# Second attention: the output product and its transposes spread over four groups, the expert weights loaded in eight parts

## Chip, cores and metric

The kernel runs on one NeuronCore of a Trainium2 chip, as one launch. The time is the device time of the whole program in microseconds (us), the median over runs. Before the change it is 1635.58 us (three runs, 1625.13 to 1639.85).

## The reference: what is computed

Two transformer-like layers run over x of shape (4 batches, 512 tokens, 256 channels), float32. Layer 0 is a modulated attention, a Mamba block and a quantised linear layer. Layer 1 is a softmax attention with 16 heads of 16 channels, and then a mixture of eight experts (hidden size 512, all experts computed for every token). The change sits in the attention of layer 1, and in the load of the expert weights that the last part needs:

```python
qkv = x @ Wqkv                       # x: the conditioned input, (4, 512, 256)
...
attn = jnp.einsum('bqhd,bkhd->bhqk', q, k)
attn = jax.nn.softmax(attn, axis=-1)
z = jnp.einsum('bhqk,bkhd->bqhd', attn, v)
z = z.reshape(b, s, d)
return z @ Wo                        # "output product"; added to x
...
h = gelu(einsum('nd,edh->neh', xf, w1) + b1)     # experts
y = einsum('neh,ehd->ned', h, w2) + b2
```

## The kernel before, in words

Each engine has its own instruction stream, written out by hand, and the engines meet at semaphores. Nothing reorders the work: what stands where in each stream is the schedule. PE is the matrix engine (matmuls and transposes into PSUM, whose eight banks are `ps[:, 0..7, :]`), ACT and DVE work on what PE made, SP issues the transfers, POOL prepares values.

The second attention goes batch by batch (`b` 0 to 3), and in each batch by four groups of four heads (`hg` 0 to 3; `g = 4 b + hg`). A group has eight steps (`j` 0 to 7), and in each step PE does, in `attend`:

- two transposed score products for this group (L1329, into banks 3 to 5), of which ACT makes exponentials (`weigh`, L1845);
- two plain score products for the group after next (L1275, banks 0 to 2), of which DVE takes row maxima (`follow`, L2285);
- after every second step, and once at the group's end, the product of exponentials and values, `values` (L1287, bank 6). The last one of a group, in the text "the group's last value product", waits for the group's last exponential. ACT copies its result to SBUF (L1859) before it begins the next group's exponentials.

Bank 7 is shared by everything small. In each group it holds: at j = 2 the maxima turned into a row (`max_rows`, L1144), which ACT copies to `mrow` (L1835) and SP sends with a small transfer into the score operand (L772, "the row of maxima"); at j = 5 the previous group's result turned to rows (`z_rows`, L1296), which DVE normalises (L2289, L2291) at its step s = 11 of 16. PE waits for the row of maxima at the start of the next group (semaphore `max_row_in_stack`).

When all four groups of a batch are done, its output product follows, during the next batch: the normalised result is transposed in two halves (`zn_columns`, L1305), each copied by ACT (L1850) to `zn_t`; then two products with `Wo` (`attention_out`, L1312), each added to x by DVE (`attention_add`, L2297). All of these go through bank 7 too. Before the change all of it is done in the group hg = 1 of the next batch, which in the text is called **the loaded group**; a group without any of it is **a plain group**. The last batch has its first transposed half in its own last group, and the rest behind the attention.

SP's stream (`feed`) sends per group the row of maxima and then, when the group's last transposed score product is done, twelve loads of heads for the next batch (L632, 64 KB each), and in batch 0 at hg = 2 one transfer of the expert weights (L780, `fw[:, cut_at:]`, 128 partitions x 16384 floats, 8.39 MB). Batches 1 and 2 are one hardware loop on every engine. The experts' stage, behind the attention, begins with waits for these weights (L1374, L2318).

## Time and profile before

| what | value |
|---|---|
| median of three runs | 1635.58 us (1625.13 to 1639.85) |
| the profiled execution's own time | 1633.18 us |
| span of the profiled execution | 1631.4 us |
| PE busy | 1454.8 us, 89% of the span |
| ACT busy, DVE busy | 855.9 us, 1067.1 us |
| share of the DMA engines taken by the transfers | 15.7% |
| second attention | about 935.7 to 1187.8 us |
| expert stage | from about 1213 us to the end |

The page gives the whole program. The change touches only the second attention, so the rows below come from queries on that stretch: instructions in order of time on one engine, with the idle time before them in square brackets and what ended it; and busy time, granted clock of PE and DMA traffic in chosen stretches. The expert stage and all before 935 us have the same instructions in both kernels.

### The profile page before, as it was taken

The page shows a single profiled execution, that of the slowest core. Times are in us where ns is not written, and L with a number is a line of the kernel's source. Part 1 is how long each engine was busy: PE and PEld are TensorE (multiplying, and loading weights), DVE is VectorE, ACT ScalarE, POOL GpSimd, SP SyncE. Part 2 cuts the span into 40 slices and gives each one's busy share as a digit, 9 for nine tenths or more (in the row PEclk, how much of TensorE's full clock was granted, in tenths as well). Part 3 has the DMA queues.
Part 4 walks back from the last instruction along what each step waited for, and adds up shares of the span by engine and source line. Part 5 has one row for each costly group of instructions (what it writes and reads, how often), then busy time and mean ns, then how long its engine had stood idle before and what let it go on. Part 6 is the DMA issues. An engine that isn't in the chain of part 4 may idle for free.

```text
span 1631.4 us, 20342 instructions
## 1 busy us (share of the span) xinstructions
PE 1454.8 (89%) x7408; PEld 994.1 (61%) x7420; DVE 1067.1 (65%) x1216; ACT 855.9 (52%) x1511; POOL 477.4 (29%) x140
## 2 busy tenths in 40 slices
PE   5898797589898989989998796889899999999997
PEld 3666342388797979643444332333258888888886
DVE  6995586589898988763344575667364565465655
ACT  2432465599898998532333385668734333333332
POOL 0998210079798888200333210000000000000000
PEclk7899998799999999978999998999998999999999
DMA  6100011302322211410203036112000000000000
GB/s 263 56 25 1 1 52 59 137 31 88 117 89 93 79 52 52 146 21 20 58 39 107 20 94 241 48 42 56 1 1 0 1 14 1 1 13 1 13 1 13
DMA packets 35616, 87.61 MB, mean 54 GB/s; under 512 B 8238, under 2 KB 24836, under 8 KB 32836
## 3 DMA queue, kind: packets, MB, share of 16 engines
q1 hardware_dynamic: 35524, 86.39, 15.7%
q8 instruction: 57, 0.93, 0.2%
q14 instruction: 35, 0.29, 0.1%
HBM read 68.10 MB, written 18.21 MB: 53 GB/s over the span
## 4 chain that ended last, share of the span: by engine, by line
PE 53%; ACT 3%; DVE 2%; issue 2%; DMA 1%; DVEq 1%; ACTq 0%
PE ps L1412 12%; PE ps L1421 12%; PE ps L1287 4%; PE ps L1154 3%; PE ps L1329 3%; PE ps L1275 2%; PE ps L1180 2%; PE ps L1116 2%; ACT arena L1845 2%; PE ps L986 1%; DMA arena<-mrow 1%; PE ps L580 1%; PE ps L1312 1%; PE ps L1038 1%; PE ps L1188 1%
## 5 line engine op out<-in xcount | busy, mean ns | idle before, releaser
L2494 POOL TENSOR_TENSOR arena<-arena 128x2048 f32<-128x2048 f32 x63 | 287.3, 4583 | 168.5 <-DVE arena L2053 168.1
L2053 DVE TENSOR_TENSOR_SCAN arena<-arena,ps 128x1024 f32<-128x1024 f32 x128 | 284.2, 2272 | 45.0 <-ACT arena L1688 22.4
L1412 PE MATMUL ps<-arena 128*128 128x256 f32 x896 | 215.5, 387 | 3.3 <-DVE early L2439 1.9
L1412 PEld LDWEIGHTS ps<-arena 128*128 128x128 f32 x896 | 172.2, 193 | 30.0 <-DVE early L2439 3.1
L1845 ACT ACTIVATE arena<-ps,rho 128x512 f32<-128x512 f32 x256 | 158.2, 689 | 59.3 <-PE ps L1329 58.3
L1688 ACT ACTIVATE arena<-arena,mam 128x511 f32<-128x511 f32 x256 | 166.2, 712 | 34.1 <-DVE arena L2053 34.1
L2285 DVE TENSOR_REDUCE mxs<-ps 128x1 f32<-128x512 f32 x224 | 141.2, 684 | 58.8 <-PE ps L1275 57.0
L974 PE MATMUL ps<-early,arena 128*128 128x128 f32 x768 | 129.7, 277 | 18.3 <-DVE arena L2053 17.9
L1878 ACT ACTIVATE hT<-hT,arena 128x256 f32<-128x256 f32 x192 | 85.7, 502 | 86.4 <-DVE hT L2443 54.9
L2474 POOL TENSOR_TENSOR arena<-arena 128x4096 f32<-128x4096 f32 x16 | 115.0, 7190 | 43.6 <-DVE arena L1972 43.6
L1676 ACT ACTIVATE arena<-arena,early 128x512 f32<-128x512 f32 x192 | 124.1, 711 | 0.1
L986 PE MATMUL ps<-early,arena 128*128 128x128 f32 x1024 | 121.5, 272 | 0.9 <-POOL arena L2494 0.7
L1421 PE MATMUL ps<-hT,arena 128*128 128x256 f32 x512 | 121.2, 380 | 0.0
L986 PEld LDWEIGHTS ps<-early,arena 128*128 128x128 f32 x1024 | 113.5, 140 | 1.8 <-POOL arena L2494 1.0
L1329 PE MATMUL ps<-arena 97*128 97x512 bf16 x256 | 96.9, 387 | 17.7 <-DMA arena<-mrow 13.5
L974 PEld LDWEIGHTS ps<-early,arena 128*128 128x128 f32 x768 | 90.5, 142 | 32.0 <-DVE arena L2053 22.9
L1421 PEld LDWEIGHTS ps<-hT,arena 128*128 128x128 f32 x512 | 97.7, 191 | 13.4
L1878 ACT ACTIVATE hT<-ps,arena 128x256 f32<-128x256 f32 x64 | 26.9, 471 | 138.9 <-PE ps L1412 138.9
L975 PE MATMUL ps<-arena 128*128 128x128 f32 x512 | 99.4, 276 | 0.0
L1421 PE MATMUL ps<-mam,arena 128*128 128x256 f32 x384 | 93.3, 379 | 0.0
L2439 DVE TENSOR_TENSOR early<-mam,ps 128x512 f32<-128x512 f32 x32 | 22.0, 687 | 101.1 <-PE ps L1412 101.1
L1275 PE MATMUL ps<-arena 96*128 96x512 bf16 x224 | 86.1, 384 | 0.0
(344 smaller groups left out, 2318.7 us busy)
## 6 DMA issues: line engine op xcount, KB each, us to landing
arena<-bc_scratch SPq DMA_DIRECT2D x32, 512.0 KB, 3.7
batch_scratch<-arena SPq DMA_DIRECT2D x2, 3072.0 KB, 9.1
arena<-batch_scratch SPq DMA_DIRECT2D x6, 1024.0 KB, 6.9
arena<-q_scratch SPq DMA_DIRECT2D x96, 64.0 KB, 2.2
arena<-k_scratch SPq DMA_DIRECT2D x96, 64.0 KB, 2.2
arena<-in_dec_w SPq DMA_DIRECT2D x1, 3855.0 KB, 16.3
arena<-in_cond SPq DMA_DIRECT2D x1, 3739.5 KB, 11.4
arena<-in_ids SPq DMA_DIRECT2D x4, 768.0 KB, 7.9
```

The costliest lines, as they stand in the source:

```text
L974: pe.transpose(ps[:, FEED + m, t * P:(t + 1) * P], dub[:, k % 2, t, m * P:(m + 1) * P], ident)
L986: last = pe.matmul(ps[:, t, m * P:(m + 1) * P], state[:, k % SLOTS, m, t * P:(t + 1) * P], ident, start=False, stop=(k % NS == NS - 1 and ...
L1275: pe.matmul(ps[:, (hg + s) % 3, :], q[0:STACK, i, qc * P:(qc + 1) * P], k[0:STACK, i, :], start=True, stop=True).then_inc(s_s_mm, 1)
L1329: pe.matmul(ps[:, 3 + (hg + n) % 3, :], k[0:STACK + 1, i, kc * P:(kc + 1) * P], q[0:STACK + 1, i, :], start=True, stop=True).then_inc(s_t_ ...
L1412: done = pe.matmul(ps[:, bank, i * S // 2:(i + 1) * S // 2], weights[:, f, :], x, start=first and i == 0, stop=last and i == 1, skip_group ...
L1421: done = pe.matmul(ps[:, bank, half * S // 2:(half + 1) * S // 2], weights[:, f, :], x[:, i, :], start=(r == 0 and half == 0 and i == 0), ...
L1676: act.activation(dub[:, k % 2, t, :], duT[b % 2][:, t, :], ACT.Copy, scale=bt[:, b, t, n:n + 1])
L1688: last = act.activation(decay[:, (2 * k + h) % 3, i, 1:S], dt[b % 2][:, m, 1:S], ACT.Exp, scale=a_neg[:, m * NS + n:m * NS + n + 1])
L1845: act.activation(pt[:, j % 4, i], ps[:, 3 + (hg + n) % 3, :], ACT.Exp, scale=rho[:, 0:1]).then_inc(s_pt, 1)
L2053: dve.tensor_tensor_scan(half, view(decay[:, (2 * k + h) % 3], [[1, 2 * S]]), view(ps[:, FEED + 2 * h, :], [[1, 2 * S]]), 0.0, ALU.mult, A ...
L2285: dve.tensor_reduce(mxs[:, hg % 2, qc, i:i + 1], ps[:, (turn + s) % 3, :], AX, ALU.max).then_inc(s_max, 1)
L2494: pool.tensor_tensor(state[:, k % SLOTS], state[:, k % SLOTS], view(c_rows[:, j % 2, k % G, :], [[0, M], [1, S]]), ALU.mult).then_inc(s_hc, 1)
```

## The change

Five things are different.

1. The output product of a batch and its transposes are spread over four groups, each at j = 7, between the group's last scores and its last value product: the first transposed half at hg = 3 of the batch itself, the second at hg = 0 of the next batch, the two products with `Wo` at hg = 1 and hg = 2. In the last batch's last group the first half stays at j = 2.
2. ACT's two copies of the transposed halves move to j = 0 of hg = 0 and hg = 1 (behind the first two exponentials), and DVE's two additions to s = 2 of hg = 2 and hg = 3 (behind the third maximum).
3. PE's waits at j = 2, 3, 5 and 7 follow: each use of bank 7 waits for the one before it.
4. The expert weights come as eight transfers of 128 x 2048 floats (1.05 MB), one behind the twelve loads of heads of each group of batches 1 and 2. The waits at the expert stage count to eight of them.
5. SP's stream is written out for all four batches instead of a loop for batches 1 and 2. The other engines keep their loop.

The diff:

```diff
@@ block.sync @@
             cut_at = FFN["w1"][0]
+            EW_LOADS = (B - 2) * HG
+            EW_PART = (FFN_W - cut_at) // EW_LOADS
...
                     if not last:
                         sp.wait_ge(s_t_mm, g * 16 + 16)
-                        if isinstance(b, int) and hg == 0:
+                        if b == 0 and hg == 0:
                             sp.wait_ge(s_q_out, 16 * B + 1)
                             sp.wait_ge(s_k_out, 16 * B + 1)
                         load_heads(sp, b + 1, hg, Q_STACK, K_STACK)
-                        if isinstance(b, int) and hg == HG - 2:
-                            sp.dma_start(fw[:, cut_at:], t_in["ffn"][:, cut_at:]).then_inc(s_ew, 16)
-
-            feed(0, False)
-            with sp.Fori(1, B - 1) as b:
-                feed(b, False)
-            feed(B - 1, True)
+                        if 1 <= b < B - 1:
+                            part = slice(cut_at + ((b - 1) * HG + hg) * EW_PART, cut_at + ((b - 1) * HG + hg + 1) * EW_PART)
+                            sp.dma_start(fw[:, part], t_in["ffn"][:, part]).then_inc(s_ew, 16)
+
+            for b in range(B):
+                feed(b, b == B - 1)
@@ block.tensor, attend @@
                         if j % 2 == 0 and j:
                             values(b, hg, kc - 1)
-                        if j < 2 and hg == 1 and not first:
-                            zn_columns(b - 1, j)
                         if j == 2 and final and hg == HG - 1:
+                            pe.wait_ge(s_x3, b * C + 1)
                             zn_columns(b, 0)
                         elif j == 2:
-                            if hg == 1 and not first:
-                                pe.wait_ge(s_znt, b * C + 1)
-                            elif not (first and hg == 0):
+                            if not first:
+                                if hg < 2:
+                                    pe.wait_ge(s_znt, b * C + hg)
+                                else:
+                                    pe.wait_ge(s_x3, (b - 1) * C + hg)
+                            elif hg:
                                 pe.wait_ge(s_zn, g)
                             max_rows(b + (hg + 1) // HG, (hg + 1) % HG)
-                        if j in (3, 4) and hg == 1 and not first:
-                            pe.wait_ge(s_mrow, g + 3)
-                            attention_out(b - 1, j - 3)
                         if j == 5 and not (first and hg == 0):
                             if not (final and hg == HG - 1):
                                 pe.wait_ge(s_mrow, g + 3)
                             else:
                                 pe.wait_ge(s_znt, b * C + 2)
-                            if hg == 1:
-                                pe.wait_ge(s_x3, b * C + 1)
                             z_rows(*((b, hg - 1) if hg else (b - 1, HG - 1)))
+                        if j == 7 and hg == 0 and not first:
+                            zn_columns(b - 1, 1)
+                        if j == 7 and hg in (1, 2) and not first:
+                            pe.wait_ge(s_zn, g + 1)
+                            attention_out(b - 1, hg - 1)
+                        if j == 7 and hg == HG - 1 and not final:
+                            pe.wait_ge(s_zn, g + 1)
+                            zn_columns(b, 0)
                     values(b, hg, TILES - 1)
...
-            pe.wait_ge(s_ew, 16)
+            pe.wait_ge(s_ew, 16 * (B - 2) * HG)
@@ block.scalar, weigh @@
-                        if hg == 1 and j in (1, 2) and not first:
-                            act.wait_ge(s_zn_tr, (b - 1) * C + j)
+                        if hg < 2 and j == 0 and not first:
+                            act.wait_ge(s_zn_tr, (b - 1) * C + hg + 1)
                             act.wait_ge(s_wo_mm, (b - 1) * C + 1)
-                            act.activation(zn_t[:, j - 1, :], ps[:, 7, :], ACT.Copy).then_inc(s_znt, 1)
+                            act.activation(zn_t[:, hg, :], ps[:, 7, :], ACT.Copy).then_inc(s_znt, 1)
@@ block.vector, follow @@
-                        if s in (7, 9) and hg == 1 and not first:
-                            attention_add(b - 1, (s - 7) // 2)
+                        if s == 2 and hg >= 2 and not first:
+                            attention_add(b - 1, hg - 2)
...
-            dve.wait_ge(s_ew, 16)
+            dve.wait_ge(s_ew, 16 * (B - 2) * HG)
```

How this moves instructions is shown at three places. In these rows the names in brackets are the semaphores waited for. The first is SP's stream from the end of group 1 of batch 0. Before:

```order
L772 DMA arena<-mrow 1x4x512
L632 DMA arena<-q_scratch 16x4x512 x6
L632 DMA arena<-k_scratch 16x4x512 x6
L780 DMA arena<-in_ffn 128x16384
L772 DMA arena<-mrow 1x4x512
L632 DMA arena<-q_scratch 16x4x512 x6
L632 DMA arena<-k_scratch 16x4x512 x6
```

and the change, from the row of maxima behind the loads of group 2 of batch 0 up to the second part of the weights:

```order
L774 DMA arena<-mrow 1x4x512
L632 DMA arena<-q_scratch 16x4x512 x6
L632 DMA arena<-k_scratch 16x4x512 x6
L774 DMA arena<-mrow 1x4x512
L632 DMA arena<-q_scratch 16x4x512 x6
L632 DMA arena<-k_scratch 16x4x512 x6
L783 DMA arena<-in_ffn 128x2048
L774 DMA arena<-mrow 1x4x512
L632 DMA arena<-q_scratch 16x4x512 x6
L632 DMA arena<-k_scratch 16x4x512 x6
L783 DMA arena<-in_ffn 128x2048
```

The one transfer of 128 x 16384 between two rows of maxima is gone; from batch 1 on, a part of 128 x 2048 stands behind each twelve loads and ahead of the next row of maxima.

The second is PE in the group hg = 1 of the loop body, around the first product with `Wo` (L1312 before, L1313 now). Before, it stands behind j = 3, its bank released by ACT's copy of the row of maxima:

```order
L1327 REGISTER_ALU
L1329 MATMUL ps<-arena 128x512 [waits exp_scores_ready]
L1273 REGISTER_ALU
L1275 MATMUL ps<-arena 128x512 [waits max_ready]
L1346 REGISTER_ALU
L1310 REGISTER_ALU [waits zn_copied,max_row_ready]
L1312 MATMUL ps<-hT,arena 128x512 [waits x3_ready]
L1312 MATMUL ps<-hT,arena 128x512
L1327 REGISTER_ALU
L1329 MATMUL ps<-arena 128x512 [waits exp_scores_ready]
```

Now it stands behind the last scores of the group (j = 7), ahead of the group's last value product (L1288) and the first score of the next group:

```order
L1328 REGISTER_ALU
L1330 MATMUL ps<-arena 128x512 [waits exp_scores_ready]
L1274 REGISTER_ALU
L1276 MATMUL ps<-arena 128x512 [waits max_ready]
L1311 REGISTER_ALU [waits zn_copied,z_normalised]
L1313 MATMUL ps<-hT,arena 128x512 [waits x3_ready]
L1313 MATMUL ps<-hT,arena 128x512
L1282 REGISTER_ALU
L1288 MATMUL ps<-arena 32x512 [waits exp_scores_ready]
L1288 MATMUL ps<-arena 32x512 x3
L1330 MATMUL ps<-arena 128x512 [waits exp_scores_ready,max_row_in_stack]
```

It moved from the middle of the group to its end, and its bank is now released by DVE's normalisation (`z_normalised`).

The third is ACT at the start of the last batch, groups 0 and 1 (the copies to `zn_t` are L1850 before, L1856 now; L1859 and L1865 copy the value product). Before, both copies are in group 1:

```order
L1845 ACTIVATE arena<-ps,rho 128x512 [waits value_products,scoreT_products] x8
L1835 ACTIVATE mrow<-ps 4x512 [waits max_row_in_stack,max_transposed]
L1845 ACTIVATE arena<-ps,rho 128x512 [waits value_products,scoreT_products] x8
L1859 ACTIVATE hT<-ps 128x512 [waits z_transposed,value_products]
L1845 ACTIVATE arena<-ps,rho 128x512 [waits value_products,scoreT_products] x4
L1850 ACTIVATE hT<-ps 128x512 [waits attention_out_products,zn_transposed]
L1845 ACTIVATE arena<-ps,rho 128x512 [waits value_products,scoreT_products] x2
L1850 ACTIVATE hT<-ps 128x512 [waits attention_out_products,zn_transposed]
L1845 ACTIVATE arena<-ps,rho 128x512 [waits value_products,scoreT_products] x2
L1835 ACTIVATE mrow<-ps 4x512 [waits max_row_in_stack,max_transposed]
```

and now there is one in each of the two groups, behind two exponentials:

```order
L1851 ACTIVATE arena<-ps,rho 128x512 [waits value_products,scoreT_products] x2
L1856 ACTIVATE hT<-ps 128x512 [waits attention_out_products,zn_transposed]
L1851 ACTIVATE arena<-ps,rho 128x512 [waits value_products,scoreT_products] x6
L1841 ACTIVATE mrow<-ps 4x512 [waits max_row_in_stack,max_transposed]
L1851 ACTIVATE arena<-ps,rho 128x512 [waits value_products,scoreT_products] x8
L1865 ACTIVATE hT<-ps 128x512 [waits z_transposed,value_products]
L1851 ACTIVATE arena<-ps,rho 128x512 [waits value_products,scoreT_products] x2
L1856 ACTIVATE hT<-ps 128x512 [waits attention_out_products,zn_transposed]
L1851 ACTIVATE arena<-ps,rho 128x512 [waits value_products,scoreT_products] x6
```

One of the two copies moved a group earlier, and both stand ahead of the third exponential.

## Rows read from the trace of the kernel before

**Rows 1.** Page, part 1: the span.

```profile
span 1631.4 us, 20342 instructions
```

**Rows 2.** Busy time by stretch: the second and third batch of the attention.

```profile
core 0: us, PE busy (x) PEld busy (x) DVE busy (x) ACT busy (x) POOL busy (x), PEclk, DMA share, GB/s
...
988.80:1066.70 77.90, 58.66 (x309) 20.12 (x306) 43.87 (x74) 44.64 (x74) 1.61 (x4) 0.89 0.29 97
1066.70:1127.90 61.20, 55.51 (x308) 18.95 (x304) 43.58 (x74) 44.15 (x74) 1.61 (x4) 1.00 0.19 52
```

**Rows 3.** PE in order of time, around the stall.

```profile
987.82 1.07 PE L1287 MATMUL ps<-arena 128*32 128x512 f32 x8 [0.70 <-ACT arena L1845]
1002.43 0.61 PE L1329 MATMUL ps<-arena 97*128 97x512 bf16 x1 [13.55 <-DMA arena<-mrow]
```

**Rows 4.** SP's DMA queue in order of time; blocks of loads and single rows.

```profile
979.05 0.42 SPq L780 DMA_DIRECT2D arena<-in_ffn  x1
982.12 0.58 SPq L772 DMA_DIRECT2D arena<-mrow  x1
...
1054.34 2.72 SPq L632 DMA_DIRECT2D arena<-k_scratch  x6
1059.96 0.60 SPq L772 DMA_DIRECT2D arena<-mrow  x1
```

**Rows 5.** DMA issues: KB each, median us to landing (attention).

```profile
arena<-q_scratch SPq DMA_DIRECT2D x78, 64.0 KB, 2.1
...
arena<-in_ffn SPq DMA_DIRECT2D x1, 23.0
```

**Rows 6.** Busy time by stretch: the output product after the stall.

```profile
1026.00:1030.00 4.00, 3.71 (x5) 1.37 (x6) 0.00 (x0) 0.17 (x1) 0.00 (x0) 0.57 0.00 1
```

**Rows 7.** PE in order of time: the end and start of plain groups.

```profile
1065.66 1.06 PE L1287 MATMUL ps<-arena 128*32 128x512 f32 x8 [0.70 <-ACT arena L1845]
1066.66 0.39 PE L1329 MATMUL ps<-arena 97*128 97x512 bf16 x1
...
1069.80 1.07 PE L1287 MATMUL ps<-arena 128*32 128x512 f32 x8
```

**Rows 8.** PE in order of time: the loaded group of the third batch.

```profile
1079.10 1.06 PE L1287 MATMUL ps<-arena 128*32 128x512 f32 x8 [0.70 <-ACT arena L1845]
...
1080.98 0.60 PE L1305 MATMUL ps<-early,hT 128*128 128x128 f32 x4
1081.42 0.38 PE L1329 MATMUL ps<-arena 97*128 97x512 bf16 x1
...
1083.69 0.66 PE L1305 MATMUL ps<-early,hT 128*128 128x128 f32 x4 [1.23 <-ACT hT L1850]
...
1086.56 0.60 PE L1144 MATMUL ps<-early,mxs 128*4 128x128 f32 x4 [0.35 <-ACT hT L1850]
...
1089.27 1.98 PE L1312 MATMUL ps<-hT,arena 128*128 128x512 f32 x4 [1.24 <-ACT mrow L1835]
1091.09 0.38 PE L1329 MATMUL ps<-arena 97*128 97x512 bf16 x1
```

**Rows 9.** ACT in order of time: a group's start.

```profile
1066.80 0.60 ACT L1859 ACTIVATE hT<-ps 128x512 f32<-128x512 f32 x1 [1.19 <-PE ps L1287]
1067.33 3.58 ACT L1845 ACTIVATE arena<-ps,rho 128x512 f32<-128x512 f32 x6
```

**Rows 10.** DVE in order of time: idle after six maxima, then an addition.

```profile
1071.87 2.48 DVE L2285 TENSOR_REDUCE mxs<-ps 128x1 f32<-128x512 f32 x4 [0.88 <-PE ps L1275]
...
1091.39 0.69 DVE L2297 TENSOR_TENSOR xT<-ps,xT 128x512 f32 x1 [2.47 <-PE ps L1312]
```

**Rows 11.** PE in order of time: ends of groups, last batch.

```profile
1126.95 1.07 PE L1287 MATMUL ps<-arena 128*32 128x512 f32 x8 [0.70 <-ACT arena L1845]
...
1161.12 1.07 PE L1287 MATMUL ps<-arena 128*32 128x512 f32 x8 [0.70 <-ACT arena L1845]
...
1173.88 1.06 PE L1287 MATMUL ps<-arena 128*32 128x512 f32 x8 [1.14 <-ACT arena L1845]
...
1186.75 1.06 PE L1287 MATMUL ps<-arena 128*32 128x512 f32 x8 [1.14 <-ACT arena L1845]
```

## Prediction, on record before the changed kernel ran

> **What bounds the kernel now.** I read the second attention in four steps. First its batches as stretches of busy time: the second and the third do the same work, but the second is longer, at a mean granted clock of 0.89 against 1.00 and with 97 GB/s of transfers against 52 [rows 2]. The reader is to see that something happens to the second that is not its work. Then PE in order of time: one wait of 13.55 us for a transfer of the row of maxima [rows 3], and, in the loaded group, waits of 1.23, 0.35 and 1.24 us for ACT [rows 8], which plain groups don't have. Then SP's queue, which tells why the row was late. Then ACT and DVE in order of time at the start of a group, where the moved instructions land.
>
> **Plain groups.** I measure a group from the start of one last value product to the next. 1065.66 to 1079.10 is 13.44 us [rows 7, 8]. PE waits in it in two places: 0.70 us ahead of the last value product, for ACT's last exponential, and from the start of the group, 1066.66, to the first value product, 1069.80, it goes at ACT's pace: ACT copies the value product (its next instruction starts 0.53 us later) and makes the exponentials at some 0.6 us each (six in 3.58 us) [rows 7, 9]. Between, from 1069.80 on, PE has no idle. So whatever delays the first four exponentials delays the group, and PE has 0.70 us free at its end.
>
> **Part 1, the weights in eight parts.** The 8.39 MB transfer starts at 979.05 and takes 23.0 us; the row of maxima is issued at 982.12, behind it, and PE gets it at 1002.43 [rows 3, 4, 5]. Batch 1 runs from 987.82 to 1065.66, 77.84 us; batch 2 from 1065.66 to 1126.95, 61.29 us [rows 3, 7, 11]. The difference, 16.55 us, is the stall of 13.55 us and what it does to PE's clock: PE begins again at the lower level (0.63 us where 0.39 is usual) and has the lower level once more in 1026 to 1030, mean 0.57 [rows 3, 6, 7]. All 16.55 us should go. What comes in its place: eight parts of 1.05 MB, at the same rate 23.0 / 8 = 2.9 us each. In the stretch 1054 to 1060 the last six loads of a block are issued until 1054.34 + 2.72 = 1057.06; the part would go out there (its issue takes 0.42 us), be through by about 1060 to 1061, and the row of maxima is issued at 1059.96 [rows 4]. PE needs that row at 1066.66 [rows 7], 6.7 us after its issue; a 64 KB load lands in 2.1 us [rows 5], so some 4 us are left. SP is busy 0.42 us longer in a gap of 1059.96 - 1057.06 = 2.9 us. I take 0 for the eight waits. Their bounds are 0 and 2.0 us each, worked out with a part that moves at the pace of the head loads around it (twelve of 64 KB issued in 2 x 2.72 = 5.4 us, some 145 GB/s, so 7.2 us for a part): it is through at 1064.3, the row lands at 1066.4 or, with one more load's landing, 2.1 us later, at 1068.5. 0 is nearer to the row of the big transfer, which is of the same kind. The last part goes out at the end of batch 2 and has the whole last batch, some 55 us, before anyone waits for it: 0. The heads of the next batch stand ahead of the part in their block, and are behind no part but the one of the group before, which is through long before: 0.
>
> Of the split the Trainium skill has a rule that speaks against it: "DMA: Bandwidth & Descriptors", section "Anatomy of one DMA", gives each transfer a fixed cost of about 2.0 us beside its bytes, whatever its size. By it seven more transfers are 14 us more, and if they stood on the path the gain would be an estimated 15 us instead of the 29 of the sum below. The trace shows the landing time (2.1 us) but also that loads of 64 KB are issued six in 2.72 us, so they overlap.
>
> **Part 2, what leaves the loaded group.** It costs 61.29 - 4 x 13.44 = 7.5 us per batch over four plain groups. Of this, PE's own work is 2 x 0.44 us for the transposes (1080.98 to 1081.42) and 2 x 1.82 us for the products (1089.27 to 1091.09), 4.5 us; the other 3.0 us are the three waits, 1.23 + 0.35 + 1.24 = 2.82 [rows 8], and small change.
>
> **Part 3, what the four groups get instead.** The two transposes, 0.44 us each, now stand in the 0.70 us in which PE is free ahead of the last value product: 0. The two products, 1.82 us each, stand in the same place: 0.70 hidden, 1.12 left, 2.24 us per batch. The last value product is that much later, and behind it ACT's copy and the next group's exponentials, all by the same 1.12 us, so it is counted once. ACT's two copies stand ahead of the third exponential, where PE goes at ACT's pace: 0.53 us each (the copy of the value product, the nearest row [rows 9]), 1.06 us per batch, not hidden; the bounds are 0, if ACT's idle later in the group gave it back, and 0.63. DVE's additions, 0.69 us [rows 10], stand behind the third maximum; DVE has 0.88 us idle behind the sixth, and the maxima that it delays are needed three products later: 0, bounds 0 and 0.69. The new waits: those at j = 2 are for a copy or an addition that stands five steps of ACT or DVE earlier than PE's seventh score product; the one at j = 7 is for a normalisation that DVE begins at step 11 of 16, with three maxima behind it that PE's last score product needs anyway. 0 for both. A batch then takes 4 x 13.44 + 2.24 + 1.06 = 57.06 us.
>
> **The last batch** runs from 1126.95 to 1186.75, 59.80 us [rows 11]. Its last two groups have no score products ahead and take 1173.88 - 1161.12 = 12.76 and 12.87 us, with 1.14 us free at the end. Now: 13.44 + 0.53, then 13.44 + 0.53 + 1.12, then 12.76 + (1.82 - 1.14 = 0.68), then 12.87, in all 55.37 us.
>
> **The sum.** Batch 1: 77.84 - 57.06 = 20.8. Batch 2: 61.29 - 57.06 = 4.2. Last batch: 59.80 - 55.37 = 4.4. Together 29.4 us, of which 16.55 from the weights and 12.9 from the spreading. The profiled execution took 1633.18 us, 1.8 us more than its span of 1631.4 [rows 1]; 1633.2 - 29.4 = 1603.8. The median of the runs shown is 2.4 us above the profiled one, and they differ among themselves by 15 us, so I add nothing for it beyond rounding: **1604 us**.
>
> **The rivals.**
>
> *Forecast, 0.68:* both parts work as priced, 1597 to 1612 us. The width is the bounds of part 3, -3.2 us for the copies and +4.1 us for six additions of 0.69, and what the clock does by chance.
>
> *The spreading gives nothing, 0.12.* ACT is as near to being the bound as PE: at each group's start PE waits for it, and the products now delay ACT's copy of the value product. If PE starts each such group with a wait and the copies cost twice their time (the exponentials behind them lose the overlap), the 12.9 us shrink to between 0 and 5: 1612 to 1617 us. Against it: the order in a group is the same for all engines from the last value product on, so a delay there should not grow.
>
> *More than forecast, 0.12.* The copies are hidden (3.2 us) and half of the rest of the products too, 1593 to 1597 us; or the execution has one drop of the clock less outside the attention.
>
> *Each transfer's landing is on the path, 0.04.* The row of maxima waits for the landing of the part ahead of it, and the slack of 4 us is not there. Seven landings of 2.1 us [rows 5] are 14.7 us: 1619 us. It is what the fixed cost in the Trainium skill's "DMA: Bandwidth & Descriptors" would do here. The overlap of the head loads speaks against it.
>
> *Slower than before, 0.04.* The row of maxima is behind a part in each of eight groups, where it was behind one transfer once. From the row's issue PE can wait 6.7 us without harm. If the parts, mixed with the head loads of 16 x 4 pieces, are so slow that the row lands 15 us after its issue, each group stalls 8.3 us, 66 us in all, against 29: 1670 us. The point from which it decides is a landing 10.4 us after the issue (29.4 / 8 = 3.7 us of stall each). For it: this very wait did happen. Against it: it took eight times the bytes, and of the 20.2 us between the row's issue and PE's start almost all was the big transfer.
>
> **How the numbers follow.** The range reaches from the better case to the case in which the spreading gives nothing: **1594 to 1618 us**, which leaves out some 0.1 to 0.15. A measurement of this kernel can tell about 1% (16 us) from no change; faster by over 1% is below 1619 us. That takes in the first three cases and half of the fourth: 0.93. Within 1%: 0.04. Slower: 0.03.
>
> **What the changed profile would show.** The wait of PE for the row of maxima is gone or below 1 us in all groups, and the granted clock is 1.00 throughout the attention. The weights land as eight transfers in about 3 us each (with the queue ahead of them perhaps 5). Plain groups still take 13.4 us; groups with hg = 1 about 15.1, hg = 2 about 14.6, hg = 0 about 14.0, hg = 3 about 13.4. The waits for the copies ahead of L1306 and L1145 and for the row copy ahead of L1313 are gone; the 0.70 us ahead of the last value product is gone in hg = 1 and 2 and shorter in hg = 0 and 3. The expert stage takes what it took. The prediction would be wrong if the row of maxima is waited for in the groups of batches 1 and 2, if the groups with a product grow by more than 1.8 us, or if the expert stage waits for its weights.

## Result, and the profile after

The changed kernel takes **1610.86 us** (median of four runs, 1609.13 to 1615.05) beside 1637.28 us for the kernel before on the same chip (four runs, 1625.13 to 1639.85): a ratio of 0.9868, 95% interval 0.9819 to 0.9917. It was measured twice more among the experiments, at 1603.47 us (0.9823, 0.9797 to 0.9850) and 1603.38 us (0.9846, 0.9804 to 0.9887). The forecast was 1604 us in a range of 1594 to 1618.

The first profiled execution of it took 1612.12 us, against 1633.18 before. Page, part 1:

```profile
span 1610.3 us, 20214 instructions
...
PE 1461.8 (91%) x7408; PEld 999.7 (62%) x7420; DVE 1066.7 (66%) x1216; ACT 855.1 (53%) x1511; POOL 477.2 (30%) x140
```

The span is 21.1 us shorter than before [rows 1], where the sum of the forecast was 29.4. Where the missing 8 us are is read from six stretches of both kernels: batch 0 from its first score product, batches 1 to 3 each from last value product to last value product, from there to the layer's modulated product (L1396 before, L1402 after), and the rest. Of the kernel before (columns: stretch and its length, busy time of each engine with its instructions, granted clock, share of the DMA engines, GB/s):

```profile
935.70:987.80 52.10, 49.30 (x276) 16.32 (x276) 41.32 (x70) 42.27 (x71) 6.88 (x8) 1.00 0.43 137
...
1126.90:1186.70 59.80, 49.78 (x272) 16.20 (x272) 26.53 (x47) 43.74 (x74) 0.40 (x1) 1.00 0.05 14
1186.70:1198.20 11.50, 10.56 (x44) 5.63 (x45) 9.65 (x11) 1.19 (x2) 0.00 (x0) 1.00 0.01 2
1198.20:1631.40 433.20, 421.63 (x1921) 363.29 (x1919) 240.20 (x374) 145.31 (x305) 0.00 (x0) 0.98 0.02 6
```

(Batches 1 and 2 are [rows 2], whose stretches begin 1 us later.) And of the change:

```profile
938.00:992.50 54.50, 52.20 (x280) 17.39 (x280) 41.74 (x70) 42.75 (x71) 6.85 (x8) 0.95 0.26 74
992.50:1049.00 56.50, 55.01 (x304) 19.23 (x304) 43.40 (x75) 43.81 (x75) 1.60 (x4) 1.00 0.37 113
1049.00:1105.50 56.50, 55.06 (x304) 19.23 (x304) 43.38 (x75) 43.83 (x74) 1.60 (x4) 1.00 0.43 131
1105.50:1161.70 56.20, 50.51 (x268) 16.09 (x268) 26.50 (x47) 43.42 (x74) 0.40 (x1) 0.97 0.11 34
1161.70:1175.50 13.80, 13.75 (x44) 6.93 (x45) 9.44 (x11) 1.19 (x2) 0.00 (x0) 0.75 0.01 2
1175.50:1610.30 434.80, 423.31 (x1921) 364.63 (x1919) 240.48 (x374) 145.01 (x305) 0.00 (x0) 0.97 0.02 6
```

The three batches take 169.2 instead of 198.9 us, 29.75 less, where the forecast had 29.4. They begin and end at these value products:

```profile
992.57 1.06 PE L1288 MATMUL ps<-arena 128*32 128x512 f32 x8 [0.26 <-ACT arena L1851]
...
1161.75 1.06 PE L1288 MATMUL ps<-arena 128*32 128x512 f32 x8 [1.14 <-ACT arena L1851]
```

But batch 0 takes 54.5 us at a mean clock of 0.95 instead of 52.1 at 1.00, though its work is the same but for one transposed half at its end, and the first score product had come 2.3 us late before it; the stretch behind the last batch takes 13.8 instead of 11.5 us at 0.75; and the rest 434.8 instead of 433.2. That is 2.3 + 2.5 + 2.3 + 1.6 = 8.7 us given back, in stretches whose instructions the change does not touch, but for that half. The 2.5 us of batch 0 are all in its first group, 14.38 us in place of 11.91. In all the profiles of this document the first score product stands anywhere between 929.65 and 938.00 us, behind the same code, so the 2.3 us are within that scatter.

The first two groups of batch 1, on PE in order of time. The rows of L1288 that are quoted are the groups' last value products; in between stands the product with `Wo`:

```profile
1006.45 1.06 PE L1288 MATMUL ps<-arena 128*32 128x512 f32 x8 [0.26 <-ACT arena L1851]
...
1019.25 0.38 PE L1276 MATMUL ps<-arena 96*128 96x512 bf16 x1
1019.47 1.88 PE L1313 MATMUL ps<-hT,arena 128*128 128x512 f32 x4
1021.28 1.06 PE L1288 MATMUL ps<-arena 128*32 128x512 f32 x8
1022.28 0.39 PE L1330 MATMUL ps<-arena 97*128 97x512 bf16 x1
```

L1313 begins as soon as the last score product is issued, 1.81 us go by, and the value product follows without idle. What stood ahead of it before, 0.70 us of idle [rows 7], is used up. The group takes 1021.28 - 1006.45 = 14.83 us. The row of maxima is no longer waited for. In SP's queue the part stands between the loads and the row, which is issued at 1014.63 and needed at 1022.28:

```profile
1008.25 2.77 SPq L632 DMA_DIRECT2D arena<-k_scratch  x6
1011.06 0.43 SPq L783 DMA_DIRECT2D arena<-in_ffn  x1
1014.63 0.58 SPq L774 DMA_DIRECT2D arena<-mrow  x1
```

and the eight parts land in 4.9 us each, in the median (DMA issues, KB each, us to landing):

```profile
arena<-in_ffn SPq DMA_DIRECT2D x8, 1024.0 KB, 4.9
```

ACT at the start of batch 1, where a copy of a transposed half (L1856) stands behind two exponentials:

```profile
993.70 0.60 ACT L1865 ACTIVATE hT<-ps 128x512 f32<-128x512 f32 x1 [1.19 <-PE ps L1288]
994.19 1.26 ACT L1851 ACTIVATE arena<-ps,rho 128x512 f32<-128x512 f32 x2
995.33 0.61 ACT L1856 ACTIVATE hT<-ps 128x512 f32<-128x512 f32 x1
995.81 2.44 ACT L1851 ACTIVATE arena<-ps,rho 128x512 f32<-128x512 f32 x4
```

The next exponential starts 0.48 us after the copy.

### The profile page after: what moved, and what is told of

Read it like the earlier page. It is cut to its first block, busy times and chain, and to the rows that moved or that the text cites. A ratio compares the mean times of both kernels' runs of the same rounds, so it can differ in the third digit from the quotient of the medians.

```text
span 1610.3 us, 20214 instructions
## 1 busy us (share of the span) xinstructions
PE 1461.8 (91%) x7408; PEld 999.7 (62%) x7420; DVE 1066.7 (66%) x1216; ACT 855.1 (53%) x1511; POOL 477.2 (30%) x140
## 4 chain that ended last, share of the span: by engine, by line
PE 55%; ACT 2%; DVE 2%; issue 2%; DVEq 1%; ACTq 0%
PE ps L1418 13%; PE ps L1427 12%; PE ps L1288 4%; PE ps L1155 3%; PE ps L1330 3%; PE ps L1276 2%; PE ps L1181 2%; PE ps L1117 2%; ACT arena L1851 1%; PE ps L987 1%; PE ps L580 1%; PE ps L1313 1%; PE ps L1039 1%; PE ps L1189 1%; PE ps L1167 1%
## 5 line engine op out<-in xcount | busy, mean ns | idle before, releaser
L1851 ACT ACTIVATE arena<-ps,rho 128x512 f32<-128x512 f32 x256 | 158.3, 689 | 27.7 <-PE ps L1330 26.5
## 6 DMA issues: line engine op xcount, KB each, us to landing
arena<-in_dec_w SPq DMA_DIRECT2D x1, 3855.0 KB, 16.4
arena<-in_cond SPq DMA_DIRECT2D x1, 3739.5 KB, 11.5
```

The costliest lines, as they stand in the source:

```text
L1851: act.activation(pt[:, j % 4, i], ps[:, 3 + (hg + n) % 3, :], ACT.Exp, scale=rho[:, 0:1]).then_inc(s_pt, 1)
```

## Experiments

Times are medians of six runs beside the kernel before on the same chip, or a single run where the text says so; a single run has no interval. A trace shows one of a kernel's runs, not its median. "Attention" is the time from the end of batch 0 to the end of the last batch, the three batches that the change is about; for the kernel before it is 198.93 us and for the change 169.18.

**parts_only: the weights in eight parts, the output product left in the loaded group.**

```diff
 # the kernel before, with the change's SP stream and its counts:
-                        if isinstance(b, int) and hg == HG - 2:
-                            sp.dma_start(fw[:, cut_at:], t_in["ffn"][:, cut_at:]).then_inc(s_ew, 16)
...
+                        if 1 <= b < B - 1:
+                            ...
+                            sp.dma_start(fw[:, part], t_in["ffn"][:, part]).then_inc(s_ew, 16)
...
-            pe.wait_ge(s_ew, 16)
+            pe.wait_ge(s_ew, 16 * (B - 2) * HG)
...
-            with sp.Fori(1, B - 1) as b:
-                feed(b, False)
+            for b in range(B):
+                feed(b, b == B - 1)
```

> The weights in eight parts alone; the output product stays in the loaded group. Theory A (the two parts of the change add up, and what is missing from the forecast is the clock outside the attention): the stall of 13.5 us and its clock loss go, batch 1 takes 61.3 us like batch 2, 16.5 us less in the attention, about 1620 us. Rival B (the eight parts cost something by their landings): batches 1 and 2 take over 62 us each, 1624 us or more.

1614.63 us, ratio 0.9898 (0.9871 to 0.9925). The ends of batch 0 and of the last batch:

```profile
984.94 1.07 PE L1288 MATMUL ps<-arena 128*32 128x512 f32 x8 [0.70 <-ACT arena L1846]
...
1167.27 1.06 PE L1288 MATMUL ps<-arena 128*32 128x512 f32 x8 [1.14 <-ACT arena L1846]
```

Attention 182.33 us, 16.60 less than before, where the forecast had 16.55. Batches 1 and 2 take 61.24 and 61.28 us. Rival B falls. (This edit also writes SP's loop out; one_late_load below, which is written out too and has one transfer, has the wait, so it is not the writing out that removes it.)

**spread_only: the output product spread, the weights as one transfer in batch 0.**

```diff
 # the change, with SP's stream of the kernel before:
-                        if 1 <= b < B - 1:
-                            ...
+                        if isinstance(b, int) and hg == HG - 2:
+                            sp.dma_start(fw[:, cut_at:], t_in["ffn"][:, cut_at:]).then_inc(s_ew, 16)
...
 # (and the loop for batches 1 and 2 and the counts of 16 as before)
```

> The spreading alone; the weights come as one transfer in batch 0 as before. Theory A: the stall of 13.5 us is still there, batches 2 and 3 take 56.4 us each, 13 us less in the attention than before, 1624 us. Rival C (the spreading brings a drop of the granted clock behind the attention, about 3.5 us, that the kernel before did not have): 1628 us, with the drop between the last group and the modulated product of layer 1 in this kernel and not in the one with the parts alone.

1610.33 us, ratio 0.9855 (0.9819 to 0.9891). Attention 182.53 us, with a wait of 12.86 us for the row of maxima:

```profile
1003.67 0.60 PE L1329 MATMUL ps<-arena 97*128 97x512 bf16 x1 [12.86 <-DMA arena<-mrow]
```

Further, batch 2 takes 56.49 us, the last 54.83. Batch 0 takes 54.57 us. From the end of the last batch to the modulated product it takes 13.82 us, as with the change, and behind that 426.50 us, 6.6 less than before. The attention takes 16.4 us less, not 13: batch 1 has 71.21 us where it had 77.84, which is 1.7 to 1.8 us more than the other batches gained (4.8 and 5.0), because no second drop of the clock followed the stall (its hg = 1 takes 14.84 us); and the other batches gained more than expected. The median is 14 us below the 1624 expected. In the trace, whose run took 1614.35 us, the gain of 18.8 us over the profile of before is made of 16.4 in the attention, 6.6 behind the modulated product and 0.5 ahead of the attention, less 2.5 in batch 0 and 2.3 behind the last batch. That the median is another 4 us lower no trace explains. As for rival C: the drop behind the last group is in this kernel (13.82 us) and not in the one with the parts alone (11.50), as it has it.

**after_again: the change once more.** No edit.

> The changed kernel once more, unaltered. Theory A (drops of the clock in the unchanged code are chance): the drop at the attention's start (4.5 us by the value product of the first group) and the one behind its last group (3.4 us) are there in some executions only; 1610 us. Rival C: the drop behind the last group is there again, and none at the start.

1603.47 us, ratio 0.9823 (0.9797 to 0.9850). Its profile, of a run of 1609.00 us, the slowest of the six, has the same drops as the first: 54.59 us in batch 0, 14.74 us in hg = 2 of the last batch where 13.26 is its time at full clock (spread_only), 13.81 us behind the last batch. At this point rival C stood better than theory A, also for the start: the four profiles with the spreading (with copy_later below) had 54.6 us in batch 0, the two without had 52.1.

**copy_later: ACT's two copies one step later.**

```diff
-                        if hg < 2 and j == 0 and not first:
+                        if hg < 2 and j == 1 and not first:
```

> As the change, but ACT's copies of the transposed halves stand one step later (j = 1, behind the fourth exponential instead of the second). Theory A: PE's first value product of the group waits for the fourth exponential only, and the copy then runs beside that product's 1.0 us; the 0.5 us per copy go, groups hg = 0 take 13.4 instead of 13.9 us and hg = 1 14.3 instead of 14.8, 3 us less than the change in all, 1608 us. Rival D (ACT is the bound of the whole group): the copy costs the same 0.5 us wherever it stands, 1611 us.

1602.44 us, ratio 0.9796 (0.9756 to 0.9836), against 1603.47 for the change on the same chip: no difference that the intervals allow. But the attention takes 166.37 us instead of 169.2, each with one drop of the clock in the last batch, and it has the expected mechanism. Behind the last batch it has no drop (11.51 us). PE in order of time, groups hg = 3 of batch 0 and hg = 0 of batch 1:

```profile
988.93 1.06 PE L1288 MATMUL ps<-arena 128*32 128x512 f32 x8 [0.26 <-ACT arena L1851]
...
993.02 1.07 PE L1288 MATMUL ps<-arena 128*32 128x512 f32 x8
994.02 0.60 PE L1145 MATMUL ps<-early,mxs 128*4 128x128 f32 x4
...
1002.32 1.06 PE L1288 MATMUL ps<-arena 128*32 128x512 f32 x8 [0.26 <-ACT arena L1851]
```

The group takes 1002.32 - 988.93 = 13.39 us, a plain group's time, where the change takes 13.88. The first value product comes 4.09 us after the group's mark in place of 4.58, and `max_rows` (L1145) follows it at once. On ACT the copy now stands behind four exponentials (L1851), and it is done within that value product:

```profile
990.06 0.60 ACT L1865 ACTIVATE hT<-ps 128x512 f32<-128x512 f32 x1 [1.19 <-PE ps L1288]
990.55 2.41 ACT L1851 ACTIVATE arena<-ps,rho 128x512 f32<-128x512 f32 x4
992.83 0.62 ACT L1856 ACTIVATE hT<-ps 128x512 f32<-128x512 f32 x1
993.31 1.30 ACT L1851 ACTIVATE arena<-ps,rho 128x512 f32<-128x512 f32 x2
994.87 1.26 ACT L1851 ACTIVATE arena<-ps,rho 128x512 f32<-128x512 f32 x2 [0.26 <-PE ps L1330]
```

The copy's 0.48 us is taken from ACT's idle time ahead of the seventh exponential, 0.26 us where the plain group has 0.74. Rival D falls.

**one_late_load: the weights as one transfer, in batch 1.**

```diff
-            EW_LOADS = (B - 2) * HG
+            EW_LOADS = 1
...
-                        if 1 <= b < B - 1:
+                        if 1 <= b < B - 1 and ((b - 1) * HG + hg) % 8 == 0 and ((b - 1) * HG + hg) // 8 < EW_LOADS:
...
 # (which leaves b = 1, hg = 0; the two counts follow)
```

> As the change, but the weights come as one transfer of 8.39 MB, behind the loads of batch 1, hg = 0. Theory A (the row of maxima waits because it stands behind the big transfer in SP's queue, whatever the batch): PE waits some 13 us for the row at the start of the third group of batch 1, with clock loss about 15 us more than the change in the attention. Rival E (the stall of the kernel before came from the store and load traffic of batch 0): no wait.

One run, 1619.05 us. PE waits for the row of maxima at the start of the group after next, as expected:

```profile
1033.56 0.61 PE L1331 MATMUL ps<-arena 97*128 97x512 bf16 x1 [12.34 <-DMA arena<-mrow]
```

The transfer lands in 24.6 us. The attention takes 182.15 us, 13.0 more than with eight parts, where 15 were expected. Rival E falls: it is the long transfer ahead of the row, not batch 0.

**four_parts: parts of 2.1 MB in every other group.**

```diff
-            EW_LOADS = (B - 2) * HG
+            EW_LOADS = 4
...
+                        if 1 <= b < B - 1 and ((b - 1) * HG + hg) % 2 == 0 and ((b - 1) * HG + hg) // 2 < EW_LOADS:
...
 # (the two counts follow)
```

> As the change, but four parts of 2.1 MB, one in every other group of batches 1 and 2. The part goes out 9.6 us before PE needs the row of maxima behind it; at the rate of the single transfer (8.39 MB in 23.0 us) it takes 5.8 us, at that of the eight parts (1.05 MB in 4.9 us) 9.8 us. Theory A: no wait of PE for the row, groups as in the change (13.4 to 14.8 us). Rival F (a part lands as slowly per byte as the eight did, and the landing of the row comes on top): a wait of some 2 us in each of four groups.

One run, 1609.99 us. Attention 169.16 us and no wait, the same as with eight. Each part lands in 7.3 us, between the two rates:

```profile
arena<-in_ffn SPq DMA_DIRECT2D x4, 2048.0 KB, 7.3
```

With 1.05 MB in 4.9, 2.1 MB in 7.3 and 8.39 MB in 24.6 us, the landing is, by an estimate from these three, some 2.0 to 2.5 us (the head loads still ahead of it in the queue among them) and 2.3 to 2.8 us per MB. Between a part's issue and the need for the row stand 9.8 us at the least here (a part in hg = 2) and 9.6 with eight; 7.3 of them are taken here and 4.9 with eight parts. Rival F falls.

**filler: idle score products in the last two groups.**

```diff
                             if not (final and hg >= 2):
                                 scores(*ahead, n)
+                            elif n >= 2:
+                                if hg == 2 and n == 2:
+                                    pe.wait_ge(s_max, B * HG * 16 + 1)
+                                pe.matmul(ps[:, (hg + n) % 3, :], q[0:STACK, i, kc * P:(kc + 1) * P], k[0:STACK, i, :],
+                                          start=True, stop=True)
```

> As the change, and in the last batch's groups hg = 2 and 3, where no score products are ahead, PE does 28 plain score products whose results nobody reads. Rival C, in its stronger form (the clock drops behind the attention because these two groups and what follows leave PE idle too often): the drops of the last batch (1.4 us in hg = 2, 2.3 us between the last group and the modulated product) go, at the price of up to 1.3 us of PE work: 2.4 us less in the stretch from the end of batch 2 to the modulated product. Theory A (the drops are chance): they are there or not as in the change, and the stretch is 1.3 us longer when they are.

These are 14 products in each of the two groups, 28 in all. 1597.33 us, ratio 0.9799 (0.9762 to 0.9836). The drop in hg = 2 is not there (14.35 us with the filler; 13.26 without filler and drop), but it was not there without the filler either, in spread_only and one_late_load. The one behind the last group is longer: 15.35 us to the modulated product in place of 13.8, and from the end of batch 2 to that product it takes 71.9 us, 1.8 more than in the change. The stronger form of rival C falls there. The rest takes 426.45 us, 8.3 less than with the change.

**mid_products: the products with Wo at j = 3.**

```diff
-                        if j == 7 and hg in (1, 2) and not first:
-                            pe.wait_ge(s_zn, g + 1)
+                        if j == 3 and hg in (1, 2) and not first:
+                            pe.wait_ge(s_mrow, g + 3)
                             attention_out(b - 1, hg - 1)
...
+                            if hg in (1, 2) and not first:
+                                pe.wait_ge(s_x3, (b - 1) * C + hg + 1)
                             z_rows(*((b, hg - 1) if hg else (b - 1, HG - 1)))
...
-                        if s == 2 and hg >= 2 and not first:
-                            attention_add(b - 1, hg - 2)
+                        if s == 7 and hg in (1, 2) and not first:
+                            attention_add(b - 1, hg - 1)
```

> As the change, but the two products with Wo stand at j = 3 of hg = 1 and hg = 2 (behind the copy of the row of maxima) instead of j = 7, and DVE's additions at s = 7 of the same groups. Theory A (what a product costs is set by whether it fills the 0.7 us that PE is free ahead of the last value product): each costs its whole 1.82 us and the wait for the row copy, 1.2 us: hg = 1 takes 16.9 and hg = 2 16.4 us instead of 14.8 and 14.3. Rival G (the place does not matter, only that there is one use of the bank per group): 14.8 and 14.3 us.

One run, 1608.30 us. hg = 1 takes 17.09 us and hg = 2 16.54 (16.9 and 16.4 were expected). The new wait ahead of the previous group's rows costs PE no idle. Batch 1, hg = 1, on PE:

```profile
1003.52 1.07 PE L1288 MATMUL ps<-arena 128*32 128x512 f32 x8
...
1007.23 1.98 PE L1313 MATMUL ps<-hT,arena 128*128 128x512 f32 x4 [1.23 <-ACT mrow L1843]
...
1016.04 1.07 PE L1288 MATMUL ps<-arena 128*32 128x512 f32 x8 [0.70 <-ACT arena L1853]
```

The product waits 1.23 us for the row copy, costs its whole 1.8, and the 0.70 us ahead of the last value product stay empty. A product costs 16.54 - 13.40 = 3.14 us here and 0.94 at j = 7. Rival G falls: having only one extra use of bank 7 in a group is not enough, the place counts.

**before_again: the kernel before once more.** No edit.

> The kernel before, once more, for its drops of the granted clock outside the attention. Theory A (the drop at the attention's start is chance): from the first score to the end of batch 0 it takes 52.1 us or 54.6 us; either may come. Rival H (the drop at the start comes only with some of the kernels): 52.1 us again.

One run, 1630.46 us. Batch 0 takes 52.12 us, which both theory A and rival H allow. The attention takes 196.77 us, with a wait of 12.55 us for the row of maxima. In this execution the second drop of the clock after the stall (1026 to 1030 in the first, [rows 6]) did not come: the loaded group of batch 1 takes 21.04 us, not 22.75. And behind the last batch:

```profile
981.70:1057.40 75.70, 57.46 (x304) 19.70 (x304) 43.93 (x75) 44.73 (x75) 1.61 (x4) 0.91 0.32 112
...
1178.50:1193.80 15.30, 15.26 (x44) 7.76 (x45) 9.56 (x11) 1.20 (x2) 0.00 (x0) 0.67 0.01 2
1193.80:1628.70 434.90, 423.34 (x1921) 364.57 (x1919) 240.35 (x374) 145.06 (x305) 0.00 (x0) 0.97 0.02 6
```

15.3 us at a mean clock of 0.67, longer than in any profile of the change. So the drop behind the attention does not need the spreading.

**after_third: the change a third time.** No edit.

> The changed kernel a third time, for comparison on one chip with the next two. 1603 us by the second measurement, 1611 by the first. In its profile 169.2 us from the end of batch 0 to the end of the last batch, 13.8 us from there to the modulated product and 434.7 us behind it if the drops of the clock there are tied to the kernel (rival C); if they are chance (theory A), at least one of the last two numbers differs.

1603.38 us, ratio 0.9846 (0.9804 to 0.9887). This profile has neither the drop at the start nor the one in the last batch:

```profile
931.80:983.90 52.10, 49.74 (x280) 16.86 (x280) 41.24 (x70) 42.26 (x71) 6.91 (x8) 1.00 0.27 77
...
1096.90:1151.70 54.80, 48.88 (x268) 15.82 (x268) 26.48 (x47) 43.44 (x74) 0.40 (x1) 1.00 0.11 34
1151.70:1165.50 13.80, 13.71 (x44) 6.93 (x45) 9.45 (x11) 1.23 (x3) 0.00 (x0) 0.75 0.01 2
1165.50:1600.30 434.80, 423.34 (x1921) 364.62 (x1919) 240.33 (x374) 145.09 (x305) 0.00 (x0) 0.97 0.02 6
```

Batch 0 takes 52.1 us, the last batch 54.8 in place of 56.2, the attention 167.83 us. The two numbers that the expectation named are unchanged (13.81 and 434.70), so by its wording theory A is not borne out there; by the start and the last batch it is. Rival H is not borne out either: the change has had both 54.6 and 52.1 us at the start.

**filler_again and copy_filler**, beside after_third on one chip. copy_filler has the edits of filler and of copy_later.

> The kernel with the 28 idle score products in each of the last two groups, a second time, beside the change on one chip. If its gain of about 6 us over the change (1597.3 against 1603.5 on another chip) is its own, it is there again, with 426.5 us behind the modulated product instead of 434.7. If it was the chip or chance: both kernels within 2 us.

1604.64 us, ratio 0.9828 (0.9790 to 0.9866). Against 1603.38 for the change: within 2 us. The gain of 6 us did not come again, though the profile again has 426.4 us behind the modulated product, and 15.35 us ahead of it.

> Both: ACT's copies behind the fourth exponential, and the idle score products in the last batch. The copies save 3 us in the attention (measured there: 13.4 and 14.3 us for hg = 0 and 1). If both gains add: 1594 us, the fastest of all. If the clock behind the attention takes the gain back, as it did in part for the kernel with the later copies alone (1602.4 us): 1598 to 1602 us.

1603.85 us, ratio 0.9824 (0.9784 to 0.9864); one of its six runs took 3757 us, and what disturbed it is not known. The median of the other five is 1601.30. The 1594 us of the first case did not come; the 1598 to 1602 of the second fits those five. The attention takes 166.58 us against 169.44 in filler_again, hg = 0 and hg = 1 take 13.40 and 14.35 us. The 3 us of the copies are there in the trace, and not to be told from nothing in the medians. Behind the last batch it has 11.50 us, without a drop, and then 434.73. No version beats the change by more than the measurement can tell.

## Why the prediction was right

**Part 1, the weights.** Forecast 16.55 us, measured 16.60 (parts_only). Some luck is in this agreement: both are taken against the first profile of before, whose batch 1 has a second drop of the clock of 1.7 us behind the stall [rows 6]. The other three profiles with a stall (before_again, spread_only, one_late_load) don't have it, and against before_again the weights are worth 75.70 - 61.24 = 14.5 us. The cause, a small transfer issued behind a long one, is shown from both sides: the wait is there with one transfer in batch 0 (before, spread_only) and in batch 1 (one_late_load), and gone with four or eight parts. What of the long transfer holds the row up is not shown. All these transfers go through SP's one queue, and the DMA engines are about full as well (by the profile a mean share of 0.84 to 1.15 in each stretch of 5 to 6 us from 979 to 1002 in the kernel before). Whether the row would have come in time through another engine's queue was not tried. The parts landed in 4.9 us; the forecast had 2.9 for the transfer, and perhaps 5 with the queue. With the slack of 6.7 us it did not matter. The fixed cost per transfer of the Trainium skill ("DMA: Bandwidth & Descriptors", "Anatomy of one DMA"), which that section gives for transfers issued from GpSimd, while these are SP's, would have had 14 us more if it stood on the path. By four_parts a part does take an estimated 2.0 to 2.5 us beside its bytes, so the trace agrees as to the landing, and all of it is hidden.

**Parts 2 and 3, the spreading.** Forecast 12.9 us; parts_only against the change gives 182.33 - 169.18 = 13.15 us, with one drop of the clock of 1.4 us in the last batch of the change (hg = 2, 14.67 us in place of 13.26). Against after_third, which has none, it is 14.5. So the mechanism came as forecast, each priced term was put a little too dear, and the near equality of 29.75 and 29.4 is in part two errors that cancel: batches 1 and 2 gained 21.4 and 4.8 us (forecast 20.8 and 4.2), the last one 3.6 (forecast 4.4; 4.9 in after_third). By terms:

| term | forecast | measured |
|---|---|---|
| a transposed half in the idle 0.70 us | 0 | 0 (hg = 3: 13.39 us) |
| a product with `Wo` at j = 7 | 1.12 us | 0.94 (hg = 2: 14.34) |
| ACT's copy at j = 0 | 0.53 us | 0.48 (hg = 0: 13.88) |
| both, hg = 1 | 1.65 us | 1.43 (14.83) |
| last batch, product in hg = 2 | 0.68 us | 0.50 (after_third, 13.26 - 12.76) |
| a plain group | 13.44 us | 13.40 |
| a batch | 57.06 us | 56.4 to 56.5 |
| the last batch | 55.37 us | 56.24, with the drop; 54.86 in after_third |
| the waits for the row of maxima | 0 | 0 |

The product was put 0.18 us too dear, because PE's free time ahead of the last value product is a little more than the 0.70 us of idle that the profile shows. The rows give the modelled end of a matmul, and the next one starts before it: behind the row of 1019.25, 0.38 us long, the product starts 0.22 us later. In a plain group of the kernel before, the last score product is

```profile
1125.87 0.38 PE L1275 MATMUL ps<-arena 96*128 96x512 bf16 x1
```

and the value product starts at 1126.95 [rows 11], so what is free is 1126.95 - 1125.87 - 0.22 = 0.86 us, and 1.82 - 0.86 = 0.96. The bound of 0 for the copies was within reach, as copy_later showed: the forecast took ACT to be the pace-maker up to the first value product, which is right, and the copy one step further on costs nothing.

**What was wrong** are two steps, "the granted clock is 1.00 throughout the attention" and "The expert stage takes what it took". In the first profile of the change the mean clock is 0.95 in batch 0, 0.97 in the last batch and 0.75 behind it, and the stretches outside the three batches take 8.7 us more than in the profile of before; the drop in the last batch takes 1.4 more. The forecast had no term for either. Of the change's three medians two are within 1 us of the forecast and the first is 7 us above it; the two close ones are in part luck, since one kernel's runs differ by more than that (1625 to 1640 us before; 1602 to 1615 us in the third measurement of the change).

Are these losses the change's own? Their times in all 14 profiles, in us:

| | without the spreading (3) | the change (3) | other kernels with it (8) |
|---|---|---|---|
| batch 0 | 52.1 three times | 54.6, 54.6, 52.1 | 54.6 four times, 52.1 four times |
| drop in hg = 2 or 3 of the last batch | none | two | two (four_parts, copy_later) |
| last batch to modulated product | 11.5, 15.35, 11.5 | 13.8 three times | 11.5 twice, 13.8 to 16.0 six times |
| behind it | 433.1, 434.8, 433.1 | 434.7 to 434.8 | 426.4 to 434.8 |

The change can run without the first two losses, and the kernel before can have a longer one of the third kind. But no kernel without the spreading has had either of the first two, in three profiles, and the third is the same in all three profiles of the change and in both of the filler. So neither is shown: that they are chance, or that they are tied to the kernel. What decides when a drop comes is open.

**The rivals.** That the spreading gives nothing is refuted by parts_only against the change: 182.33 against 169.18 us in the traces, and 1614.6 against 1603.5 us in the medians on the same chip, whose ratios to the kernel before, 0.9898 (0.9871 to 0.9925) and 0.9823 (0.9797 to 0.9850), don't touch. That each transfer's landing is on the path, and that the row is late behind each part, are refuted by the groups' times: PE waits for no row of maxima. The case "more than forecast" did not come in the change: the copies cost 0.48 us each, and only copy_later hides them.

Small slips of the working that change nothing: from the row's issue to PE's start it is 1002.43 - 982.12 = 20.3 us, not 20.2; the chances of being faster by over 1% add up to 0.94, where 0.93 is written.

## What to carry to other kernels

A small transfer that an engine waits for should not be issued behind a long one in the same queue: cut the long one so that a piece fits in the slack, and check the slack from issue to need in the trace. (Another queue for the small one was not tried here.) Look for a place for extra work on the engine that sets the time where that engine waits for another one's last result: here the same product cost 0.94 us in one such place and 3.14 in the middle of the group. A copy on the other engine can be free right behind the instruction that releases the waiting engine: 0.48 us one step earlier, nothing there. When a gain is a per cent, read it from a stretch that holds only the changed work, and take several profiles, of the kernel before too, before the rest is explained.

## What the hardware showed that I had not expected

PE's granted clock falls to the lower of its two levels (1.2 of 2.4 GHz) without any long idle of PE. In after_third the longest drop comes among the gates' 64 small products (8 columns each), of which 32 stand in 1183 to 1187 and 16 each from 1191 and from 1198 on. The stretches before and in it:

```profile
1175.00:1179.00 4.00, 4.00 (x11) 1.71 (x9) 3.66 (x2) 1.27 (x2) 0.00 (x0) 1.00 0.00 0
1179.00:1183.00 4.00, 2.64 (x12) 1.92 (x11) 0.05 (x1) 3.15 (x4) 0.00 (x0) 1.00 0.00 0
1183.00:1187.00 4.00, 4.00 (x34) 3.92 (x32) 0.64 (x1) 0.00 (x0) 0.00 (x0) 0.93 0.00 0
1187.00:1207.00 20.00, 20.00 (x66) 17.40 (x66) 7.10 (x13) 5.71 (x11) 0.00 (x0) 0.50 0.00 1
```

By the profile PE is busy all the time from 1183 on, and still has the lower level for 20 us; "busy" is from modelled ends, so it does not say how full the array is. Ahead of the drop stand a wait in 1179 to 1183 and the first 32 small products. In the second profile of the filler kernel the same instructions take 8.3 us less, with the lower level among them only here:

```profile
1188.00:1192.00 4.00, 4.00 (x32) 3.82 (x31) 0.69 (x1) 0.48 (x1) 0.00 (x0) 1.00 0.02 4
1192.00:1196.00 4.00, 4.00 (x16) 3.46 (x16) 0.00 (x0) 0.84 (x2) 0.00 (x0) 0.57 0.00 0
1196.00:1216.00 20.00, 20.00 (x109) 18.04 (x109) 11.97 (x21) 12.35 (x22) 0.00 (x0) 1.00 0.00 1
```

The "Trainium skill", in "TensorE: Matmul & The Clock Gate", section "Part 1: The HAM clock gate (the "warmup" mystery)", has the lower level as the state after idle time. The stall of 13.55 us agrees with that [rows 3], with a granted clock of 0.50 from 993 to 1002 us; this drop, with PE busy by the profile in every stretch around it but for a pause of 1.4 us, does not fit it as plainly. That the small products bring it about was not tried.
